# Loading both halves of a q window in one transfer, and the relative node numbers of four groups in another

## The reference

```python
h = relu(layernorm(x))                      # x: 6250 x 256
eq = h @ Wq + bq
ek = h @ Wk + bk
e = edge_attr @ We + be                     # edge_attr: 106250 x 256
m = relu(eq[dst] + ek[src] + e)
ft = segment_sum(m, dst, num_segments=6250)
out = x + ft @ Wr + br
```

## Time and profile before

| | |
|---|---|
| time, median of 3 runs | 1136.51 us (1132.95 to 1136.51) |
| profiled execution, first to last instruction | 1412.1 us |
| profiled execution's own time | 1412.1 us (its span; none other is given) |
| mean granted TensorE clock in it | 0.947 of full speed |
| PE / DVE / ACT / POOL busy | 1195.9 / 960.7 / 866.0 / 938.3 us |
| transfers issued by SP for windows, for relative numbers | 416, 208 |

### The profile page before, as it was taken

The page is one execution under the profiler, slowest core; times in us unless marked ns, Lnnn a source line. Parts: engine busy times, 40 slices in busy tenths (PEclk is TensorE's granted clock), DMA queues, the critical chain, the costliest instruction groups (busy, mean ns, idle before and its releaser), DMA issues.

```text
span 1412.1 us, 28721 instructions
## 1 busy us (share of the span) xinstructions
PE 1195.9 (85%) x9166; PEld 1132.3 (80%) x9166; DVE 960.7 (68%) x1382; ACT 866.0 (61%) x1569; POOL 938.3 (66%) x949
## 2 busy tenths in 40 slices
PE   9879888889888888888888888879888898788878
PEld 8868788778887787887878878878878788788877
DVE  7767677656766776667667667666666766666656
ACT  7746566556665665656565666556666656665554
POOL 8756667666666676666666667676666767666653
PEclk9979999988999999999999999999989999999999
DMA  9777777667767776777777777777777677776662
GB/s 304 220 224 228 210 228 238 211 208 220 232 211 214 227 237 210 236 208 221 224 217 242 212 216 219 214 237 228 213 211 240 219 223 216 218 235 201 205 190 88
DMA packets 171124, 309.12 MB, mean 219 GB/s; under 512 B 30817, under 2 KB 117358, under 8 KB 171038
## 3 DMA queue, kind: packets, MB, share of 16 engines
q1 hardware_dynamic: 130590, 198.79, 43.0%
q0 software_dynamic: 39888, 108.97, 28.6%
q10 hardware_dynamic: 560, 0.52, 0.1%
HBM read 281.20 MB, written 26.95 MB: 218 GB/s over the span
## 4 chain that ended last, share of the span: by engine, by line
PE 45%; ACT 19%; another core or an unknown queue 15%; issue 13%; DVE 3%; DMA 1%; SPq 1%; POOL 1%; DVEq 0%; ACTq 0%; POOLq 0%
PE p_edge L1341 26%; PE p_sum L1445 8%; ACT edge_hi L822 6%; PE p_edge L1424 4%; ACT m_hi L878 4%; ACT rel_g L867 4%; PE p_turn L1434 3%; PE p_turn L1341 1%; PE p_sum L1341 1%; ACT pick L870 1%; ACT idx L814 1%; ACT hT_hi L895 1%; DVE edge_lo L1159 1%; DVE m_lo L1193 1%
## 5 line engine op out<-in xcount | busy, mean ns | idle before, releaser
L727 POOL DMA_INDIRECT k_rows<-k_table,idx x815 | 872.9, 1071 | 436.9 <-issue 216.2
L1341 PE MATMUL p_edge<-we_hi,edge_hi 128*128 128x256 f32 x1662 | 497.4, 299 | 95.6 <-issue 49.3
L1341 PE MATMUL p_edge<-we_hi,edge_lo 128*128 128x256 f32 x1662 | 484.8, 292 | 17.3 <-issue 16.7
L1341 PE MATMUL p_edge<-we_lo,edge_hi 128*128 128x256 f32 x1662 | 483.8, 291 | 17.6 <-issue 16.8
L1184 DVE TENSOR_TENSOR p_edge<-p_edge,k_rows 128x1024 f32<-128x1024 f32 x208 | 255.8, 1230 | 288.1 <-ACT hT_hi L895 139.5
L1341 PEld LDWEIGHTS p_edge<-we_hi,edge_hi 128*128 128x128 f32 x1662 | 336.0, 202 | 119.3 <-issue 89.8
L1341 PEld LDWEIGHTS p_edge<-we_lo,edge_hi 128*128 128x128 f32 x1662 | 336.3, 202 | 23.3 <-issue 23.0
L1341 PEld LDWEIGHTS p_edge<-we_hi,edge_lo 128*128 128x128 f32 x1662 | 334.5, 201 | 25.4 <-issue 25.0
L885 ACT ACTIVATE sum_rows<-p_sum 48x256 f32<-48x256 f32 x208 | 77.6, 373 | 430.8 <-remote 266.4
L1159 DVE TENSOR_TENSOR edge_lo<-edge,edge_hi 128x1024 fp32r<-128x1024 f32 x208 | 255.1, 1226 | 55.1 <-ACT edge_hi L822 28.4
L1193 DVE SCALAR_TENSOR_TENSOR m_lo<-p_edge,m_hi 128x1024 fp32r<-128x1024 f32 x208 | 253.6, 1219 | 40.4 <-issue 30.1
(11 more groups left out here) (154 smaller groups left out, 1133.5 us busy)
## 6 DMA issues: line engine op xcount, KB each, us to landing
edge<-in_edges SPq DMA_DIRECT2D x208, 512.0 KB
rel_row<-rel_table SPq DMA_DIRECT2D x208, 96.0 KB
q_win<-q_table SPq DMA_DIRECT2D x416, 48.0 KB
k_rows<-k_table,idx POOLq DMA_INDIRECT x815
q_table<-hn SPq DMA_DIRECT2D x46, 256.0 KB
pre<-in_x SPq DMA_DIRECT2D x55, 128.0 KB
out_rows<-pre SPq DMA_DIRECT2D x55, 128.0 KB, 1.7
k_table<-k_rows SPq DMA_DIRECT2D x23, 256.0 KB, 4.3
```

The costliest lines, as they stand in the source:

```text
L727: nc.gpsimd.indirect_dma_start(out=k_rows[:, slot, j, :], out_offset=None, in_=k_table, in_offset=bass.IndirectOffsetOnAxis(ap=offsets, ax ...
L1341: ins = nc.tensor.matmul(target, a(h), b[:, h, :], start=(start and h == 0 and n == 0), stop=(stop and h == HALVES - 1 and n == 2))
```

## The change

`q_table` becomes one table in which a node's high row stands at 2 node and its low row at 2 node + 1. A window is then 96 rows in one piece, and one transfer loads it: partition 2 i gets the high row and partition 2 i + 1 the low row of node i of the window. `lane_node` follows: it is half of (partition number less its lowest bit), with one more DVE instruction for the lowest bit. The store of a q block writes the two rows of a node as one run of 2 KB.

The relative numbers of the four groups of a body are loaded by one transfer of 4 KB to each of 96 partitions, in a buffer of two bodies instead of four groups, with one semaphore instead of four. It is issued with the first group of a body. Two small prologue buffers (`br_high`, `bias_raw`) move into parts of `pre` that are free then.

```diff
-    q_table = nc.dram_tensor("q_table", (2, NODE_BLOCKS * LANES, D), F32R, kind="Internal").ap()
+    q_table = nc.dram_tensor("q_table", (2 * NODE_BLOCKS * LANES, D), F32R, kind="Internal").ap()
+    rel_bodies = rel_table.rearrange("(b u) e -> b (u e)", u=UNROLL)
-    q_blocks = q_table.rearrange("s (b p) d -> s b p d", p=LANES)
+    q_blocks = q_table.rearrange("(b p s) d -> b p s d", p=LANES, s=2)
...
-        rel_row = sb("rel_row", [2 * WIN, 4, GROUP], I16)
+        rel_row = sb("rel_row", [2 * WIN, 2, UNROLL, GROUP], I16)
...
+        br_high = pre[0:BR_LO + 1, 1, 3 * D:4 * D].bitcast(F32R)
+        bias_raw = pre[0:1, 1, 0:3 * D].rearrange("p (n d) -> p n d", d=D)
...
-                    sp.dma_start(q_blocks[:, b].rearrange("s p d -> p s d").bitcast(F32),
+                    sp.dma_start(q_blocks[b].bitcast(F32),
                                  q_parts[:, b].bitcast(F32)).then_inc(s_qfirst[v], 16)
...
-            def load_row(it, u):
-                body, slot, n, _, gb = visit(it, u)
-
-                after(sp, s_pick, n - 4)
-                g = gb * UNROLL + slot
-                sp.dma_start(rel_row[:, slot, :], rel_table[bass.ds(g, 1), :].to_broadcast([2 * WIN, GROUP]))\
-                    .then_inc(s_row[slot], 16)
+            def load_rows(it):
+                _, _, n, _, gb = visit(it, 0)
...
+                after(sp, s_pick, n - UNROLL)
+                sp.dma_start(rel_row[:, bass.ds(half, 1)].rearrange("p a u e -> p (a u e)"),
+                             rel_bodies[bass.ds(gb, 1), :].to_broadcast([2 * WIN, UNROLL * GROUP])).then_inc(s_row, 16)
...
-                for s in range(2):
-                    sp.dma_start(q_win[s * WIN:(s + 1) * WIN, slot, :].bitcast(F32),
-                                 q_table[s, bass.ds(w0, WIN), :].bitcast(F32)).then_inc(s_win[slot], 16)
+                sp.dma_start(q_win[0:2 * WIN, slot, :].bitcast(F32),
+                             q_table[bass.ds(w0 * 2, 2 * WIN), :].bitcast(F32)).then_inc(s_win[slot], 16)
...
-            for u in range(UNROLL):
-                load_row(0, u)
+            load_rows(0)
...
-                    load_row(it, u)
+                    if u == 0:
+                        load_rows(it)
...
-                act.wait_ge(s_row[slot], 16 * (body + 1))
+                act.wait_ge(s_row, 16 * (body + 1))
...
+                nc.vector.tensor_scalar(lane_id[:], lane_id[:], 1, None, ALU.bitwise_and).then_inc(s_prep, 1)
...
-                nc.vector.tensor_scalar(lane_wrap[:], lane_id[:], float(WIN), float(WIN), ALU.is_ge, ALU.mult)\
-                    .then_inc(s_prep, 1)
+                dve.wait_ge(s_prep, SPAN_STEPS + 1)
+                nc.vector.tensor_scalar(lane_wrap[:], lane_id[:], 0.5, None, ALU.mult).then_inc(s_prep, 1)
...
-                pe.wait_ge(s_win[slot], 32 * (body + 1))
+                pe.wait_ge(s_win[slot], 16 * (body + 1))
```

More of the change, by code:

```diff
@@ L119, in gnn_program @@
         lane_raw = lane_node
-        lane_id = sb("lane_id", [2 * WIN, 1], F32)
+        lane_id = sb("lane_id", [2 * WIN, 1], I32)
         src_idx = sb("src_idx", [LANES, GROUPS, TILES], I32)
@@ L275, in gnn_program @@
         s_edge = [sem(f"edge_loaded_{u}") for u in range(UNROLL)]
-        s_row = [sem(f"rel_row_loaded_{u}") for u in range(UNROLL)]
+        s_row = sem("rel_rows_of_body_loaded")
         s_win = [sem(f"q_window_loaded_{u}") for u in range(UNROLL)]
@@ L355, in gnn_program @@
         SPAN_STEPS = 2 * CHUNKS + 10
-        PREP_STEPS = SPAN_STEPS + 4 + CHUNKS + 2
+        PREP_STEPS = SPAN_STEPS + 5 + CHUNKS + 2
         def out_block(it):
@@ L865, in make_pick @@
                     act.sem_inc(s_go_act, 1)
-                nc.scalar.activation(gap[:], rel_row[:, slot, :], ACT.Abs, scale=-1.0,
+                nc.scalar.activation(gap[:], rel_row[:, bass.ds(body % 2, 1), slot, :].rearrange("p a e -> p (a e)"), ACT.Abs, scale=-1.0,
                                      bias=lane_node[:, bass.ds(ps, 1)]).then_inc(s_gap, 1)
```

17 lines of the change are left out of this document (7 added, 10 removed).

## The result

The changed kernel took **1144.91 us** (median of 4 runs, 1142.72 to 1147.81), the kernel before 1136.51 (4 runs, 1132.95 to 1138.39). The ratio is 1.0082 with a 95% interval of [1.0064, 1.0100]: slower by 0.8%, where faster was held likeliest, and 0.9 us above the top of the range. In a repeat beside other runs of the kernel before it was 1.0056 [1.0033, 1.0080]; the loss is 0.6 to 0.8%.

A forecast was written before the change was run, and what follows sets the result against it. The prediction took POOL's gathers to bound the loop in plain runs, with PE behind. It summed -5.1 us at the start and +0.2 us for DVE to -4.9, with 0 for the loop: 1136.5 to 1131.6 us, range 1120 to 1144.

The forecast's parts named there:

- What bounds the loop: Main loop: in plain runs POOL sets the pace at 1.25 us a gather, 1127 us in all, PE behind it.
- the 266.4 us: ACT's waits before `take_sum`, read as late news from PE in the profiled execution that plain runs hardly have.
- The start, -5.1 us: Prologue: SP issues the edge load 5.6 us earlier, so ACT takes message 0 at 87.6, not 92.75; -5.1 us.
- rival A: Start: gain hidden anyway, since plain SP reaches the edge load early enough; only +0.2 is left, 1136.7 us; chance 0.31.
- SP's time in the loop, 0: Main loop: 364 transfers fewer save SP 157 us, but SP waits for PE anyway; costed at 0.
- Windows, bytes and waits in the main loop, 0: Main loop: same bytes, fewer packets, one larger load of numbers; costed at 0, as all loads are a body ahead.
- Rival C: DVE's wait at L1184: gathers queue behind the 4 KB burst, a quarter of the bodies pay; 1143.6 us, slower; chance 0.21.
- Rival B: DMA engines in the loop: fewer packets help the gathers DVE waits for, 7 us more gain; 1124.6 us; chance 0.14.
- What the profile was to show: ACT's starting edge wait under 8 us, message 0 within 1.5 us, gathers at 1.25 us, row waits near 14 us.
- C's sign: Changed profile under rival C: more and longer waits for gathered rows before L1184, or ACT idle before L867.
- DVE's extra instruction, +0.2: DVE prologue: one more instruction on 96 x 1 ahead of the tables that SP and everything later wait for; +0.2 us.

The follow-up runs named there:

- experiment 11: Kernel before with `edge_low` as two instructions of 128x512: 1.0278 of the kernel before on the chip of 1388 us, 1.0003 when run again at 1137.76 us.
- experiments 9 and 10: `edge_low` moved ahead of DVE's wait for gathered rows, in the kernel before and in the changed kernel: 0.9937 and 0.9919 of the kernel before, at 1388 us.
- experiment 13: Changed kernel without the loads of relative numbers after the second body: 0.9964 of the kernel before.

## Why the prediction was wrong

**What bounds the loop: right.** POOL's 1.25 us a gather was taken from a profile in which POOL waited 203 us for ACT. In the plain profile it is the pace from end to end: 815 gathers from 86.33 to 1118.30 are 1032.0 us, of which 814 x 1.251 are 1018.3. The reading of the 266.4 us as a trait that plain runs hardly have holds for the chips on which the 1136 us were measured. On the chip of 1388 us the kernel before has no trace; the halves of experiment 11 have such waits there too (195.4 us, 65 times), the kernels of experiments 9 and 10 hardly any (7.2 us at most), so it may be more than a trait of one execution.

**The start, -5.1 us: wrong, and rival A right on it.** A said that at 0.43 us a step SP reaches the edge load early enough even now. It does: the plain SP issues the eight windows in 6.05 us, not 13.40, and `edge_hi` is there before the addition ends. SP issues the edge load 3.0 us earlier after the change (74.91 for 77.94), not 5.6, and the gain is 0: this execution's start is even 1.2 us later, of which 0.3 are left by 98 us. A's time, 1136.7 us, is 8 us too low all the same, since A too has 0 for the loop.

**SP's time in the loop, 0: right.** SP's waits for PE before its window loads grow from 317.5 to 476.0 us, by 158 us: the 157 us that it no longer spends on transfers have become waiting.

**Windows, bytes and waits in the main loop, 0: the step that failed.** "All loads are a body ahead" is true of who waits for these loads: in the loop nobody does. But the gathers have no lead at all, and how the loads go out shifts their landings (25 late ones to 49 and 35). That it does so on the DMA engines, 90% busy in the loop where I had priced them from the 1% of the chain in the earlier trace rows, is likely and not shown. The term was 0 in the sum, and it is +6.5 us of held gathers in the profiled execution (+3.8 in the repeat). The packet count fell by 26.7 thousand, where I had 21.4: I had left out the packets under 512 bytes, 5.8 thousand of them (30817 to 24994), 16 for each of the 364 transfers, and counted 50 stores of q where only the 46 of the loop became fewer packets. The queue's share stayed at 53%, so the time went by bytes, the lower end that I gave.

**Rival C: sign and place right, price by the wrong path.** It named the late landing in front of L1184 and gave 1143.6 us. It let DVE's wait be the price. That wait didn't grow (141.6 and 140.9 us). So it is luck that its 1143.6 us lies 1.3 us from the measured time. The price is paid on POOL, by `edge_low` sliding onto a gather's start, a mechanism whose row I had in hand: the gather of 1.69 us in the earlier trace rows, which I used as a figure for the base and not as a cost that the change could raise. And not the burst alone does it: either part of the change alone costs 0.4 to 0.6%, and smaller pieces cost 2.3% at a bad place.

**Rival B: wrong in its sign.** Fewer packets helped nothing. Its premise, that loads and gathers get in each other's way, fits experiment 13, where fewer bytes helped.

**What the profile was to show.** Message 0 is taken as the addition ends (86.82), and the gather pace stays at 1.25 us: as forecast. ACT's wait for the edge features under 8 us proves nothing, since it was 5.53 already in the plain profile of before. Gathered rows are waited for not 14 us but 141, before and after. C's sign, more and longer waits in front of L1184, came by half: they are longer (0.99 for 0.89 us) and fewer (142 for 160), with the same sum. That sum hides the late landings, and the single additions on the timeline show them.

**DVE's extra instruction, +0.2: not seen apart**, hidden in the shift of the start.

## What to carry to other kernels

When two engines run in step with almost no slack between them, ask of every edit what it does to the *phase* of the one against the other; transfers that nobody waits for can still shift it, here through the landing of the gathers. Merging transfers is no gain by itself where the issuing queue has time to spare, and a gather that begins under a DVE instruction with two SBUF inputs pays what is left of that instruction, less some 0.1 us. Before pricing a change from a profile, hold its span against the plain times: where they differ by a quarter, take the shares of its chain for nothing, and look for rows that would be the same in both.

## What the runs showed of the hardware

- A gather of 128 rows takes POOL 0.95 us plus 0.30 to the next, unless DVE works on two SBUF inputs as it begins. Then it ends 0.8 us after that instruction (0.83, 0.81 and 0.82 us in the three cases shown, the last with the 0.35 us of `send`). With a one-input instruction of the same 1.21 us at the same place none of 815 takes over 1.13 us. An instruction with one input in PSUM holds none: in the changed kernel 194 gathers begin with over 0.2 us of an addition (L1184) still to run and 159 with as much of `message_low` (L1193), and the longest of them takes 0.96 us. The Trainium skill ("SBUF — State Buffer", Who interferes with whom) gives the rule: DVE and GpSimd share a pair of ports under an exclusive lock, two SBUF inputs of DVE contend with a GpSimd instruction that reads SBUF, and whichever issues second waits for the first to end. The runs agree for the gather that comes second: it ends only after `edge_low` has. They don't agree the other way round: at 612.10 `edge_low` begins 0.06 us behind a gather and takes its usual 1.22 us. A gather seems to need the port near its start alone. The same section has a `tensor_tensor` leave a descriptor-generating DMA alone, for a reason that it marks as inferred; for a gather, which reads its row numbers from SBUF, the 1.94 us shows the opposite, and the measurement decides.
- One chip took 1380 to 1395 us for a kernel that others run in 1132 to 1142.
- A median gather takes 0.946 us in some executions and 0.949 in others, of one and the same kernel too; over 815 that is 2.4 us, more than a fourth of what was measured here, and part of no held time in the table.
- What stays open: why the windows' layout makes rows late while the relative numbers are loaded (neither the number of its transfers nor the length of the stores' runs does), where loads and gathers meet, and which placing of the loads would be best.
